# Sparsemax thresholds by Newton steps on eight heads at a time, in a cross-attention and FFN kernel

## What is computed

```python
def sparsemax(x):
    x = x - jnp.max(x, axis=-1, keepdims=True)
    zs = -jnp.sort(-x, axis=-1)
    rho = jnp.arange(1, L + 1, dtype=x.dtype)
    cssv = jnp.cumsum(zs, axis=-1) - 1.0
    support = zs > cssv / rho
    k = jnp.maximum(jnp.sum(support, axis=-1, keepdims=True), 1)
    tau = jnp.take_along_axis(cssv, k - 1, axis=-1) / k.astype(x.dtype)
    return jnp.clip(x - tau, 0.0)
...
scores = jnp.einsum('bhqd,bhkd->bhqk', qh, kh) * scale
attn = sparsemax(scores)
out = jnp.einsum('bhqk,bhkd->bhqd', attn, vh)
...
real = jnp.einsum('bti,io->bto', x, jnp.cos(theta + theta_noise))
imag = jnp.einsum('bti,io->bto', x, jnp.sin(phi + phi_noise))
return jnp.sqrt(real * real + imag * imag)
...
x = x + attention(_layernorm(x), ctx, ctx)
x = x + ffn(_layernorm(x))
```

## Time and profile before

| | us |
|---|---|
| median of 3 runs | 843.59 |
| lowest, highest | 840.98, 843.95 |
| the profiled execution | 843.08 |
| its span in the trace | 840.8 |
| busy in the span: PE, DVE, ACT, POOL | 657.9, 629.0, 454.7, 181.9 |
| granted clock of PE, mean | 0.886 of full speed |

### The profile page before, as it was taken

The page is one execution under the profiler, slowest core; times in us unless marked ns, Lnnn a source line. Parts: engine busy times, 40 slices in busy tenths (PEclk is TensorE's granted clock), DMA queues, the critical chain, the costliest instruction groups (busy, mean ns, idle before and its releaser), DMA issues.

```text
span 840.8 us, 16547 instructions
## 1 busy us (share of the span) xinstructions
PE 657.9 (78%) x4960; PEld 423.0 (50%) x4960; DVE 629.0 (75%) x4046; ACT 454.7 (54%) x872; POOL 181.9 (22%) x147
## 2 busy tenths in 40 slices
PE   3796824778887779898888979997759979995485
PEld 2463613644466445664467536744447446742351
DVE  3699994699936997599929993899629994999401
ACT  2262745554486454874498438854538447842441
POOL 5710530002420034202420152015300152000000
PEclk9898765889889789999899989998979989997698
DMA  9610100000020000200020002000020000000000
GB/s 311 231 49 1 72 1 1 3 2 0 11 92 1 0 11 1 92 0 0 10 93 0 0 10 92 1 0 10 1 91 0 0 10 13 3 1 10 11 2 10
DMA packets 9806, 26.25 MB, mean 31 GB/s; under 512 B 2090, under 2 KB 2090, under 8 KB 8686
## 3 DMA queue, kind: packets, MB, share of 16 engines
q1 hardware_dynamic: 9710, 25.35, 8.7%
HBM read 23.71 MB, written 1.64 MB: 30 GB/s over the span
## 4 chain that ended last, share of the span: by engine, by line
DVE 70%; issue 10%; PE 8%; DMA 5%; DVEq 3%; SPq 2%; ACT 2%; ACTq 0%
DVE cand L743 22%; DVE cand L755 17%; DVE top L750 14%; DMA xq<-in_x 3%; DVE csum L765 2%; PE work L333 2%; PE work L338 2%; PE tps L406 2%; DMA out_y<-att 2%; DVE topz L761 2%; DVE gk L768 1%; SPq L193 1%; DVE g_max L771 1%; DVE st L718 1%; DVEq L830 1%
## 5 line engine op out<-in xcount | busy, mean ns | idle before, releaser
L743 DVE MAX8 cand<-S 100x8 f32<-100x60 f32 (+1 forms) x1536 | 191.0, 205 | 43.5 <-issue 25.4
L406 PE MATMUL tps<-ident,S 100*128 100x100 f32 x768 | 102.9, 276 | 80.6 <-DVEq L835 46.6
L390 PE MATMUL work<-kT,qz 128*100 128x361 f16 x768 | 151.7, 339 | 0.8 <-ACT k_f L565 0.8
L581 ACT ACTIVATE S<-S,neg_tau 100x722 f32<-100x722 f32 x128 | 114.3, 895 | 69.8 <-DVE neg_tau L773 69.8
L755 DVE MATCH_REPLACE8 cand<-top,cand 100x96 f32<-100x96 f32 x640 | 148.1, 243 | 0.0
L750 DVE MAX8 top<-cand 100x8 f32<-100x96 f32 x768 | 139.9, 245 | 0.0
L333 PE MATMUL work<-ctxT,wk 128*128 128x361 f16 x768 | 134.1, 340 | 7.0 <-ACT k_f L565 5.7
L406 PEld LDWEIGHTS tps<-ident,S 100*128 100x128 f32 x768 | 84.7, 155 | 101.2 <-ACT pT L546 44.0
L283 POOL TENSOR_TENSOR ctxT<-ctxT_f,ctxT 128x1024 f16<-128x1024 f32 (+1 forms) x24 | 46.8, 1950 | 393.1 <-ACT ctxT L546 392.8
L333 PE MATMUL work<-wv,ctxT 128*128 128x512 f16 x576 | 125.7, 379 | 0.4 <-ACT S L546 0.4
L546 ACT ACTIVATE S<-work 100x722 f32<-100x722 f32 x128 | 99.4, 776 | 27.9 <-PE work L390 25.4
(11 more groups left out here) (99 smaller groups left out, 586.5 us busy)
## 6 DMA issues: line engine op xcount, KB each, us to landing
ctxT_f<-in_ctx SPq DMA_DIRECT2D x8, 1444.0 KB, 6.7
xq<-in_x SPq DMA_DIRECT2D x8, 200.0 KB
xr<-in_x SPq DMA_DIRECT2D x8, 200.0 KB
out_y<-att SPq DMA_DIRECT2D x8, 200.0 KB
wq<-in_L_xattn_Wq SPq DMA_DIRECT2D x1, 1024.0 KB, 9.2
S<-in_L_xattn_Wk SPq DMA_DIRECT2D x1, 1024.0 KB, 11.5
S<-in_L_xattn_Wv SPq DMA_DIRECT2D x1, 1024.0 KB, 10.8
wcos<-in_L_ffn_theta SPq DMA_DIRECT2D x1, 1024.0 KB, 12.8
```

What stands on the lines that cost most here:

```text
L390: last = nc.tensor.matmul(buf[0:L, half, 0:HALF], qz2[:, i, h // G, h % G, :], kT2[:, j, h // G, half * HALF:(half + 1) * HALF], start=(n ...
L406: last = nc.tensor.transpose(tps[:, half, c * L:(c + 1) * L], S[0:L, h, kc * P:(kc + 1) * P], ident[0:L, 0:L])
L581: nc.scalar.activation(S[0:L, h, 0:N], S[0:L, h, 0:N], ACT.Relu, bias=neg_tau[:, h:h + 1], accum_out=row_sum[:, h:h + 1]).then_inc(relu_do ...
L743: last = nc.vector.max(cand[:, j, 8 * i:8 * i + 8], S[0:L, h, cuts[i]:cuts[i + 1]])
```

## The change

DVE. The sort, scan and maximum are gone, with the tiles `top`, `topz`, `csum`, `gk`, `chain0`, `inv_k` and 58 small memsets at the start. `thresholds` is now a generator for eight heads: 48 maxima for each of two groups of four (`maxes`), a first guess from the two largest of each piece, and then four Newton steps on the candidates: one on the three largest of each piece, one on the five largest and two on all eight. One step is ten instructions. `tau_ready` counts eight heads at once. `settle` takes the flags without a bit code and loops over the eight heads in a hardware loop, with one copy of `refine` in the code instead of eight, and a register load in each turn.

The order on DVE: the first group's maxima of batch b now run ahead of `mark(b - 1, 1)`, `ln1(b + 1)` and `settle(b - 1, 1)`; `tail1` and `mark(b, 0)` stand between the maxima of the second eight heads and their Newton steps.

PE adds up the flags of part 1 after the fourth head's scores instead of after the first's. ACT runs no relu within the scores any more, takes relus 0 to 7 within the three parts of V and 8 to 15 within the last three parts of k, and does the square root of `ln1` after the eighth head's scores instead of after the first's.

```diff
@@ PE, one_pass
                         scores(b, G * g + j)
-                        if g == 0 and j == 0 and not first:
+                        if g == 0 and j == G - 1 and not first:
                             sum_flags(b - 1, 1)
...
@@ ACT
             def relu(b, h):
 
-                if h % G == 0:
-                    act.wait_ge(tau_ready, DC * b + h // G + 1)
+                if h % (2 * G) == 0:
+                    act.wait_ge(tau_ready, 2 * b + h // (2 * G) + 1)
...
                         s_of(b, G * g + j)
-                        if g == 0 and j == 0 and not first and not last:
+                        if g == 1 and j == G - 1 and not first and not last:
                             ln_sd(b + 1, mv1, sd1, ln1_stat, ln1_sd)
-                        if g == DC - 1 and not first:
-                            relu(b, j)
...
                 for i in range(NC // 2):
-                    if not first:
-                        relu(b, G + i)
                     v_of(b, i)
                     if not last:
                         ctxT_of(b + 1, i)
-                    if first:
-                        relu(b, i)
+                    for h in range(3 * i, min(3 * i + 3, 2 * G)):
+                        relu(b, h)
...
@@ DVE
+            def maxes(b, g):
 
                 dve.wait_ge(s_ready, H * b + G * (g + 1))
                 dve.sem_inc(scores_seen, 1)
...
+                for j in range(G):
+                    for i in range(PIECES):
+                        last = nc.vector.max(cand[:, G * (g % 2) + j, 8 * i:8 * i + 8],
+                                             S[0:L, G * g + j, cuts[i]:cuts[i + 1]])
+                return last
+
+            def thresholds(b, part):
+
+                dve.sem_clear(found)
                 dve.sem_clear(tau_step)
...
+                maxes(b, 2 * part)
+                if part == 0:
+                    yield
+                maxes(b, 2 * part + 1).then_inc(found, 1)
+                yield
+                pieces = cand[:, :, :].rearrange("p g (i r) -> p g i r", r=8)
...
+                for ranks in RANKS:
+                    E = PIECES * ranks
+                    t4 = tau_t[:, :].rearrange("p (g a c) -> p g a c", a=1, c=1)
...
+                    nc.vector.tensor_tensor(dif[:, :, 0:E].rearrange("p g (i r) -> p g i r", r=ranks),
+                                            pieces[:, :, :, 0:ranks], t4.broadcast_to([L, 2 * G, PIECES, ranks]),
+                                            ALU.subtract).then_inc(tau_step, 1)
...
+                    nc.vector.tensor_scalar(over[:, :, 0:E], dif[:, :, 0:E], 0.0, None, ALU.is_ge)\
+                        .then_inc(tau_step, 1)
+                    nc.vector.tensor_scalar(dif[:, :, 0:E], dif[:, :, 0:E], 0.0, None, ALU.max).then_inc(tau_step, 1)
...
+                    nc.vector.tensor_tensor(over[:, :, 0:E // 2], over[:, :, 0:E // 2], over[:, :, E // 2:E],
+                                            ALU.add).then_inc(tau_step, 1)
...
+                    nc.vector.reduce_sum(count_g[:, :], over[:, :, 0:E // 2], AX).then_inc(tau_step, 1)
...
+                    nc.vector.reduce_sum(f_sum[:, :], dif[:, :, 0:E], AX).then_inc(tau_step, 1)
...
@@ DVE, settle
-                todo = dve.value_load(flag_i[0:1, 0:1], min_val=0, max_val=2 ** (2 * G) - 1)
+                todo = dve.value_load(any_i[0:1, 0:1], min_val=0, max_val=L)
                 with dve.If(todo > 0):
-                    for n in range(2 * G):
-                        with dve.If((todo >> n) & 1 > 0):
-                            refine(2 * G * part + n)
+                    with dve.Fori(0, 2 * G) as n:
+                        rows = dve.value_load(flag_i[0:1, bass.ds(n, 1)], min_val=0, max_val=L)
+                        with dve.If(rows > 0):
+                            refine(n + 2 * G * part)
                 dve.sem_inc(verified, 1)
...
@@ DVE, one_pass
+                steps = thresholds(b, 0)
+                next(steps)
                 if not first:
                     mark(b - 1, 1)
                 if not first and not last:
                     ln1(b + 1)
                 if not first:
                     settle(b - 1, 1)
-                thresholds(b, 0)
-                thresholds(b, 1)
-                thresholds(b, 2)
+                next(steps)
+                for _ in steps:
+                    pass
+                steps = thresholds(b, 1)
+                next(steps)
                 if not first:
                     tail1(b - 1)
                 mark(b, 0)
-                thresholds(b, 3)
+                for _ in steps:
+                    pass
                 if not first:
                     sum_squares(b - 1)
                 settle(b, 0)
```

More of the change, by code:

```diff
@@ L107, in build_kernel @@
         sq = sb("sq", [L, 2, D])
-        cand = sb("cand", [L, G, NCAND])
-        top = sb("top", [L, G, TOP])
-        topz, csum, gk = (sb(n, [L, G, TOP]) for n in ("topz", "csum", "gk"))
-        chain0, inv_k = sb("chain0", [L, G, TOP]), sb("inv_k", [L, G, TOP])
-        g_max = sb("g_max", [L, G])
+        cand = sb("cand", [L, 2 * G, NCAND])
+        dif, over = sb("dif", [L, 2 * G, NCAND]), sb("over", [L, 2 * G, NCAND], BF16)
+        tau_t, f_sum, count_g = (sb(n, [L, 2 * G]) for n in ("tau_t", "f_sum", "count_g"))
+        zero = sb("zero", [L, 1])
         neg_tau = sb("neg_tau", [L, H])
@@ L115, in build_kernel @@
         flag = sb("flag", [L, 2 * G])
-        bit, flag_bits = sb("bit", [1, 2 * G]), sb("flag_bits", [1, 2 * G])
-        flag_code, flag_i = sb("flag_code", [1, 1]), sb("flag_i", [1, 1], I32)
+        flag_i, any_i = sb("flag_i", [1, 2 * G], I32), sb("any_i", [1, 1], I32)
         again = sb("again", [P, 32])
@@ L666, in one_pass @@
                 if first:
-                    relu(b, G - 1)
                     q_of(b + 1, 0)
@@ L671, in one_pass @@
                         k_of(b + 1, m)
-                        relu(b, G + m)
                     for h in range(2 * G, H):
@@ L676, in one_pass @@
                     ln_sd(b - 1, mv2, sd2, ln2_stat, ln2_sd)
-                    relu(b, 2 * G - 1)
                     if not last:
@@ L680, in one_pass @@
                         q_of(b + 1, 1)
-                    relu(b, 2 * G)
                     x2T_of(b - 1)
-                    relu(b, 2 * G + 1)
                     if not last:
                         k_of(b + 1, 0)
-                    relu(b, 2 * G + 2)
-                    relu(b, 2 * G + 3)
                     squares(b - 1)
@@ L690, in one_pass @@
                     for m in range(1, DC):
-                        relu(b, 3 * G + m - 1)
-                        if m == DC - 1:
-                            relu(b, 3 * G + m)
                         if not last:
                             k_of(b + 1, m)
+                        for h in range(2 * G + 3 * (m - 1), min(2 * G + 3 * m, H)):
+                            relu(b, h)
             passes(act, one_pass, ring)
@@ L875, in angles @@
                 dve.sem_inc(angle_ready, 1)
-            nc.vector.memset(chain0[:, :, 1:TOP], 1.0)
-            nc.vector.memset(chain0[:, :, 0:1], 0.0)
             nc.vector.memset(again[:, :], 0.0)
-            for n in range(2 * G):
-                nc.vector.memset(bit[:, n:n + 1], float(2 ** n))
-            for k in range(TOP):
-                last = nc.vector.memset(inv_k[:, :, k:k + 1], 1.0 / (k + 1))
-            last.then_inc(dve_const, 1)
+            nc.vector.memset(zero[:, :], 0.0).then_inc(dve_const, 1)
             nc.vector.memset(eps_c, LN_EPS).then_inc(dve_const, 2)
```

89 lines of the change are left out of this document (36 added, 53 removed).

## The result

The changed kernel takes 956.17 us (median of 4 runs, 954.31 to 956.65); the kernel before, run beside it, 843.77 us (840.98 to 845.39). The ratio is 1.133, 95% interval 1.130 to 1.137: 112.4 us slower. The forecast was 918 us with a range of 884 to 946, so sign and mechanism held, but the time lies 10 us above the range.

The account below looks back on a forecast made before the run. The prediction took a ring of handoffs between PE, DVE and ACT to bound each pass. Stretch changes of -14.5, +16.0, +27.9, +23.6, +3.8, +12.5 and +6.5 made +75.8 on 843.08: 918.9, forecast as 918 us, range 884 to 946.

Parts of the forecast that it names:

- sign and mechanism: Whole kernel: slower, chance 0.94, through the moved checks making PE and DVE wait; a plain pass 100.7 us against 88.9.
- The handshake: Late checks: PE idles some 7 us behind its fourth score, ln1 waits for ACT's root, transposes for settle; plain pass +11.8 us.
- The second Newton batch: DVE's thresholds for the second eight heads of a pass: 18.1 us without cover, ending 78.9 us into the pass.
- the alternative in the prediction: Newton step on DVE: the 16-bit fold gets the double rate and is the cheap operation, so a batch costs about 17.7 us.
- Refining: Flagged settle on DVE: three refined heads, each some 16 us extra instead of 11.1, bounds 11 and 22.
- The next pass's start: After the last relus: table load, four heads at 1.45 us and 1.7 for the clock, from 92.0 to 100.7 us.
- the first pass: Stretch between the first two batches' first maxima, without the handshake: 94.6 us to 80.1, so -14.5.
- the last stretch: From 716.37 to the span's end: four more relus (3.5) and the flag wait less DVE's saving, +6.5 us.
- Unflagged settle: DVE's check with no head flagged, now skipping one refine body instead of eight: 1.4 us, bounds 0.9 and 4.2.
- The rival that kept 4.2: Settle's branch stays dear: 2.8 us more in the chain of six passes, about +20, so 938 us; chance 0.14.
- Thresholds converge: Four Newton steps leave the sort's same three heads over tolerance; non-convergence, over 1,400 us if most are flagged, had chance 0.03.
- The rival on the other side: PE's flag wait ends before PE runs out of work, so DVE's saving counts: 14.5 us less a pass, some 760; chance 0.04.

Follow-up runs that it names:

- small padding: Changed kernel without refining, GpSimd's padding of q cut to 4 of 100 columns from the second pass on: 873.8 us, against 907.3 with full padding.
- the small steps moved: Changed kernel with checks early; previous batch's tail ahead of the third group's maxima, its root ahead of V's first copy, mark and sum of squares between Newton steps: 827.6 us.
- the sorts with the small steps moved: Kernel before, sorts kept; previous batch's tail ahead of the third group's maxima, its root ahead of V's first copy, sum of squares ahead of the last scan: 853.3 us.
- q ahead of V: Changed kernel with checks and small operations early, plus next q's projection ahead of V and GpSimd's padding ahead of its context split: 841.0 us.
- the fastest kernel: Changed kernel with checks and small operations early, next q projected before V, sinusoidal layer before next k, settling written out eight times: 803.6 us, 0.952 of before.

## Why the forecast was right in kind and short in size

**The handshake: right.** Step by step in the pass that begins at 502.73, forecast and measured, in us behind it: flag sum 6.1 and 6.1; the eighth S 16.0 and 16.5; root 17.5 and 18.1; settle's end 19.9 and 20.2; output projection 36.2 and 36.2; V's end 55.8 and 55.8; mark's end 60.8 and 61.0. The sums from the rows held within 0.6 us, and undoing the order alone gave back 100 us.

**The second Newton batch: the step that failed.** I took 18.1 us for either batch, with 19.6 as the upper bound, and wrote that the second has no cover. It has none, but it is 21.4 us in the six passes behind the first, and 25.9 in the first (108.43 to 134.32). That is 3.3 us a pass above the forecast where it counts, and 7.8 in the first: 28 us. Alone a batch is 15.7, below my lowest price of 17.2. The fold of the counts is the cheap operation, as the alternative in the prediction had it (384 elements 0.35 us where I had 0.57; 240 elements 0.28 for 0.44), and the ten gaps of 0.035 aren't there: a step on 768 takes 4.49 us where its operations add up to 4.61. The reduction behind the fold cost what I had (0.55 for 0.57). So two errors partly cancel, by luck: 2.4 us too dear alone, and 5.7 us of contention that I had at nothing. I had priced operations from rows where POOL was idle or where the kind of operation doesn't care, and never asked who else is at work at the place they are moved to. With small padding the time falls by 33 us; 36.6 were missing between forecast and measured change.

**Refining: somewhat short.** A flagged settle was forecast at 16 us more than an unflagged one and measured at 18.8, within the bounds of 11 and 22. The loads and turns are not what I missed: they make 4.8 more than in before (20.2 against 15.4), where I had some 5. But I had put the 16 on top of the new, cheap unflagged settle of 1.4, as if a flagged one also lost the 2.9 us of the long skip, and so had 17.4. Against the run without refining, the three stages with a refined head are 18.1, 18.2 and 8.6 us longer; the sum had 16, 16 and 5.3. That is 7.6 us of the miss.

**The next pass's start: a little short.** From the last relu to the first maxima 8.7 forecast, 9.96 measured (492.77 to 502.73). The granted clock was 0.66 in that stretch: the scores of two heads took 2.02 and 1.91 us where 1.09 is their length at full clock, and I had 1.7 us in all for the clock. Over six passes it is some 8 us.

These three terms make some 43 us together, 4.5 more than the 38.5 by which the stages exceed the forecast. Against them stand 2.5 us in the first pass, whose second batch began that much earlier than forecast (43.4 behind its first maxima for 45.9), and 0.7 in the last stretch; the rest I didn't separate.

**Unflagged settle: right.** 1.4 forecast, 1.18 to 1.3 measured where before had 4.1. The Trainium skill (Runtime: NRT & Kernel Launch, "Instruction fetch mechanics") has a stall where a branch leaves the pages fetched ahead. The trace is in line with it: a skip over one body costs less than one over eight. No run separates fetching from another cost of a long skip, though. The rival that kept 4.2 fell.

**Thresholds converge: right.** Three refined heads, in the stages 151.31, 274.47 and 608.20.

**The rival on the other side.** It said that DVE's saving counts only if PE doesn't stand behind the fourth score. It stood 7.05 us. With the checks early and nothing else moved the kernel was still above before, at 856.2; with the small steps moved as well it is 827.6, where the sorts with the small steps moved take 853.3. That the difference is DVE's saved work isn't shown by itself.

## What to carry to other kernels

Batching a step over more items halves its instructions, but whatever is queued behind it waits twice as long; count the small operations that other engines wait for, and put them between the steps of the batch. Before one operation replaces another on VectorE, look at what GpSimd runs at that place: here maxima and reductions ran beside it undisturbed, many two-input and simple one-input operations didn't, and even one on eight elements could wait for the whole of a GpSimd instruction. When a move removes a wait and the time rises, ask what the moved piece had been hiding.

## What the runs showed of the hardware

- A DVE operation kept out by POOL reads as a long operation: 0.28 us became 1.67. Even operations on 8 elements stretched (scalar_tensor_tensor 0.17 to 0.74 at 568.22, and to 1.44 with q ahead of V), while reciprocals stayed at 0.20. POOL's padding was longer too, 4.21 and 4.37 us against 3.69 and 4.01 without Newton steps beside it.
- Adding two halves of 384 bf16 elements took 0.35 us, where a subtraction over 480 f32 elements took 0.66 and one over 288 took 0.46.
- A settle whose skipped body holds one refining costs 1.2 us of "issue", one with eight 4.1; a loop with a register for the head took 5.48 us to reach the fourth body, and 1.2 us for each turn more. The same loop in the kernel with the checks early took 6.15 us to the fourth and 10.27 to the seventh, 1.4 a turn; why isn't shown.
- The granted clock in plain passes was 0.89 in after against 0.94 in before: idle stretches of PE cost a second time in the matmuls behind them (mix 2.23 against 1.24 us). In the fastest kernel it was 0.914 over the whole span, in after 0.846.
